# Reading the attention product and its maxima from PSUM, in a fused cross-attention and feed-forward kernel

## The reference, cut to what matters

```python
def reference(x, ctx_2048, W1, W2):            # x, ctx: 16 x 256 x 512 f32; W1 2048x512, W2 512x2048
    x = x + xattn(layernorm(x), ctx_2048, ctx_2048)
    x = x + ffn(layernorm(x), W1, W2)
    return x

def xattn(q, k, v):                            # 8 heads of 32 rows, over the 512 columns
    qk = einsum('bdm,bdn->bmn', qh, kh) / sqrt(32)
    return einsum('bmn,bcn->bcm', softmax(qk, axis=-1), vh)

def ffn(x, W1, W2):                            # both products with 8-bit rounded inputs, ternary weights
    h = silu(bitlinear(x, W1))
    return bitlinear(h, W2)
```

## Time and profile before

| | us |
|---|---|
| median of 3 runs | 919.39 (917.77 to 921.04) |
| the profiled execution | 921.06 |
| its span, first to last instruction | 919.0 |

### The profile page before, as it was taken

One profiled execution on the slowest core, in us unless ns is written; L12 is line 12 of the kernel. 1 busy time (PEld: TensorE's weight loads), 2 busy tenths in 40 slices (PEclk: granted clock), 3 DMA queues, 4 the chain that ended last, 5 costly groups with the idle time before them and its releaser, 6 DMA issues.

```text
span 919.0 us, 13936 instructions
## 1 busy us (share of the span) xinstructions
PE 791.9 (86%) x4580; PEld 292.9 (32%) x4580; DVE 789.7 (86%) x1624; ACT 671.6 (73%) x1089; POOL 617.5 (67%) x619
## 2 busy tenths in 40 slices
PE   1667799998999999999999999899999999989875
PEld 0322233333333333333333333333333333333222
DVE  1958799999999999999999999999999999998552
ACT  3485687877777777787777777787777778777753
POOL 4125578776777777777777777777777777875651
PEclk9977999999999999999999999999999999999997
DMA  8550333222333333312233333212233333120000
GB/s 264 156 158 18 70 81 70 61 63 63 71 81 81 82 81 70 82 47 65 63 81 81 82 81 81 70 50 67 60 79 81 81 82 81 47 58 25 24 12 23
DMA packets 49927, 68.28 MB, mean 74 GB/s; under 512 B 6336, under 2 KB 30912, under 8 KB 49344
## 3 DMA queue, kind: packets, MB, share of 16 engines
q1 hardware_dynamic: 49856, 67.39, 29.2%
HBM read 33.55 MB, written 8.39 MB: 46 GB/s over the span
## 4 chain that ended last, share of the span: by engine, by line
PE 51%; DVE 35%; issue 7%; POOL 3%; ACT 2%; DMA 1%; SPq 0%; POOLq 0%; ACTq 0%; DVEq 0%
PE bank_b L918 12%; DVE mx L703 11%; PE pv L887 9%; PE mxp L877 8%; PE st L867 7%; DVE hmx L782 6%; DVE late L777 6%; PE bank_b L956 4%; PE bank_a L956 3%; PE bank_a L908 3%; DVE cparts L713 2%; PE dn L898 1%; PE bank_a L926 1%; POOL late L492 1%; DVE sm L756 1%
## 5 line engine op out<-in xcount | busy, mean ns | idle before, releaser
L465 POOL TENSOR_TENSOR probs<-probs 128x512 f32<-128x512 f32 x256 | 332.8, 1317 | 138.5 <-PE pv L887 125.2
L703 DVE TENSOR_REDUCE mx<-mxp 128x1 f32<-128x512 f32 x512 | 338.1, 680 | 60.8 <-PE mxp L877 58.9
L546 ACT ACTIVATE probs<-st,sm 128x512 f32<-128x512 f32 x512 | 343.1, 686 | 53.0 <-PE st L867 49.8
L877 PE MATMUL mxp<-ks,qs 96*128 96x512 f16 x512 | 201.5, 395 | 56.8 <-DVE mx L703 24.9
L867 PE MATMUL st<-qs,ks 98*128 98x512 f16 x512 | 197.9, 388 | 5.3 <-DMA qs<-crow 3.1
L887 PE MATMUL pv<-probs,vt 128*32 128x512 f32 x1024 | 142.7, 630 | 0.0
L918 PE MATMUL bank_b<-w2t,late 128*128 128x512 f16 x512 | 134.7, 388 | 2.6 <-ACT late L578 2.6
L867 PEld LDWEIGHTS st<-qs,ks 98*128 98x128 f16 x512 | 50.1, 98 | 145.5 <-ACT probs L546 63.4
L877 PEld LDWEIGHTS mxp<-ks,qs 96*128 96x128 f16 x512 | 53.4, 105 | 132.1 <-DVE mx L703 65.2
L782 DVE TENSOR_REDUCE hmx<-late 128x1 f32<-128x512 f32 x128 | 84.6, 681 | 2.2
L609 ACT ACTIVATE late<-bank_a,sm 128x512 f32<-128x512 f32 x64 | 44.0, 688 | 50.4 <-PE bank_a L956 50.4
(11 more groups left out here) (92 smaller groups left out, 1024.9 us busy)
## 6 DMA issues: line engine op xcount, KB each, us to landing
xs<-x SPq DMA_DIRECT2D x32, 256.0 KB, 4.0
cs<-ctx SPq DMA_DIRECT2D x32, 256.0 KB, 4.1
ks<-kh SPq DMA_DIRECT2D x64, 128.0 KB, 3.4
qs<-qh SPq DMA_DIRECT2D x64, 128.0 KB, 3.7
xr<-x SPq DMA_DIRECT2D x32, 256.0 KB, 4.0
out<-late SPq DMA_DIRECT2D x32, 256.0 KB, 2.0
probs<-w SPq DMA_DIRECT2D x4, 1024.0 KB, 9.0
ks<-kl SPq DMA_DIRECT2D x32, 128.0 KB, 3.2
```

The lines of the kernel that those rows point to most:

```text
L465: pool.tensor_tensor(probs[:, 2 * pair, h, :], probs[:, 2 * pair, h, :], probs[:, 2 * pair + 1, h, :], ALU.add).then_inc(sum_done, 1)
L546: act.activation(probs[:, c, h, :], st[u % 2][:, :], ACT.Exp, scale=sm1[:, r, ESC:ESC + 1]).then_inc(exp_done, 1)
L703: dve.reduce_max(mx[:, slot.ring(off), NC * h + c:NC * h + c + 1], mxp[m % 2][:, :], axis=AX.X).then_inc(max_done, 1)
L877: pe.matmul(mxp[m % 2][:, :], qs[0:3 * DH, r, h, c * P:(c + 1) * P], ks[0:3 * DH, r, h, :], start=True, stop=True).then_inc(mx_done, 1)
```

## The change

- `values` c = 0 and 1 move from units 6 and 10 to units 8 and 11; `pv_evac` and `pvs` go, `attend` reads `pv`, and `values` c = 0 waits for `attended` of the tile before.
- `cparts` and `cparts_low` go. `mx` is 128 columns wide, zero beyond 16, and `ct` transposes it as f32, in unit 11 instead of 12. `ct_evac` writes the high part (f16) from bank_a, VectorE's new `ct_low` (unit 12) subtracts it from bank_a and writes the low part; bank_a is free after `ct_low`. The crow rows are two transfers.
- `sums` write a buffer of their own; they wait for `denominators` of the tile before instead of `values`. `exp` waits for `values` and for the sum that read its block.
- SyncE issues the loads first, then two transfers of `qh`, two of `kh`, one of `ql`, one of `kl`, each as soon as its half is ready.
- The memset of -1 goes from GpSimd (after the first `ql`) to VectorE's first instruction; `mx` is cleared by GpSimd at the start.
- `key_scale_b` is a tensor_scalar. Every step has its own semaphore, the leftovers of a loop form go (nothing is emitted for them before).

```diff
-    cparts=[-6],
-    ct=[-4],
+    ct=[-5],
     ct_evac=[-5],
-    values=[6, 10, 15, 18],
+    ct_low=[-4],
+    values=[8, 11, 15, 18],
-    pv_evac=[18],
...
+                if slot.has(4) and loads:
+                    load(slot, 4)
                 if slot.has(2):
-                    wait_alone(sp, st_done, slot, UNITS, 2 - RING, UNITS, passed)
-                    wait(sp, x_k_scales, slot, K_LOW, 2, K_LOW)
-                    for g, part in enumerate((kh, kl, kh)):
-                        sp.dma_start(ks[DH * g:DH * (g + 1), r, :, :], part[:, k, :]).then_inc(k_stacked[r], 16)
-                    wait(sp, x_k_operands, slot, Q_LOW, 2, Q_LOW)
-                    for g, part in enumerate((qh, qh, ql)):
-                        sp.dma_start(qs[DH * g:DH * (g + 1), r, :, :], part[:, k, :]).then_inc(q_stacked[r], 16)
+                    wait(sp, st_done, slot, UNITS, 2 - RING, UNITS)
+                    wait(sp, qh_done, slot, 1, 2, 1)
+                    for g in range(2):
+                        sp.dma_start(qs[DH * g:DH * (g + 1), r, :, :], qh[:, k, :]).then_inc(q_stacked[r], 16)
+                    wait(sp, kh_done, slot, 1, 2, 1)
+                    for g in (0, 2):
+                        sp.dma_start(ks[DH * g:DH * (g + 1), r, :, :], kh[:, k, :]).then_inc(k_stacked[r], 16)
+                    wait(sp, ql_done, slot, 1, 2, 1)
+                    sp.dma_start(qs[2 * DH:3 * DH, r, :, :], ql[:, k, :]).then_inc(q_stacked[r], 16)
+                    wait(sp, kl_done, slot, 1, 2, 1)
+                    sp.dma_start(ks[DH:2 * DH, r, :, :], kl[:, k, :]).then_inc(k_stacked[r], 16)
...
-                    wait(sp, ct_evac, slot, 1, 1, 1)
-                    sp.dma_start(qs[3 * DH:3 * DH + 2, r, :, :].rearrange("o h m -> o (h m)"), crow[:, k, :]).then_inc(c_stacked[r], 16)
+                    wait(sp, ct_low, slot, 1, 1, 1)
+                    for a in range(2):
+                        sp.dma_start(qs[3 * DH + a:3 * DH + a + 1, r, :, :].rearrange("o h m -> o (h m)"), crow[:, k, a, :]).then_inc(c_stacked[r], 16)
...
             def pair_sum(slot, off, n):
                 pair, h = divmod(n, TH)
                 if h == 0:
-                    wait_alone(pool, pv_done, slot, NC, off, 2 * pair + 1, passed)
+                    wait(pool, dn_done, slot, 2, off - 1, pair + 1)
                 wait(pool, exp_done, slot, UNITS, off, TH * (2 * pair + 1) + h + 1)
-                pool.tensor_tensor(probs[:, 2 * pair, h, :], probs[:, 2 * pair, h, :], probs[:, 2 * pair + 1, h, :],
+                pool.tensor_tensor(sums[:, pair, h, :], probs[:, 2 * pair, h, :], probs[:, 2 * pair + 1, h, :],
                                    ALU.add).then_inc(sum_done, 1)
...
-                if u % (2 * TH) == 0:
-                    wait(act, dn_done, slot, 2, -1, c // 2 + 1)
+                if h == 0:
+                    wait(act, pv_done, slot, NC, -1, c + 1)
+                wait(act, sum_done, slot, 2 * TH, -1, TH * (c // 2) + h + 1)
                 wait(act, st_done, slot, UNITS, 0, u + 1)
...
             def maximum_low(slot, off):
+                k = slot.ring(off) % 2
+                wait(dve, ct_evac, slot, 1, off, 1)
+                dve.tensor_tensor(crow[:, k, 1, :], bank_a[0:UNITS, 0:P], crow[:, k, 0, :], ALU.subtract).then_inc(ct_low, 1)
...
-                wait(dve, pv_evac, slot, 1, off, 1)
-                dve.tensor_tensor(att[:, k, :], pvs[:, k, :], rden[:, :], ALU.mult).then_inc(token_scales, 1)
+                wait(dve, pv_done, slot, NC, off, NC)
+                wait(dve, rden_done, slot, 1, off, 1)
+                dve.tensor_tensor(att[:, k, :], pv[:, :], rden[:, :], ALU.mult).then_inc(attended, 1)
...
+            dve.memset(ks[3 * DH:P, :, :, :], -1.0).then_inc(minus_ones, 1)
...
-                    wait(pe, pv_evac, slot, 1, off, 0)
+                    wait(pe, attended, slot, 1, off - 1, 1)
...
-                wait(pe, cpart_done, slot, 2, off, 2)
+                wait(pe, max_done, slot, UNITS, off, UNITS)
                 bank_free(pe, BANK_A, slot, off, place("ct", 0))
-                pe.transpose(bank_a[0:2 * UNITS, 0:P // 2].bitcast(f16), cparts[:, slot.ring(off), :, :].rearrange("p a b -> p (a b)"),
-                             idh[:, :]).then_inc(ct_done, 1)
+                pe.transpose(bank_a[:, 0:P], mx[:, slot.ring(off), :], idf[:, :]).then_inc(ct_done, 1)
```

More of the change, by code:

```diff
@@ L153, in wait @@
     value = slot.at(per_tile, off, more)
-    assert not slot.looped or per_tile * (slot.b + off) + more > 0
-    if slot.looped or value > 0:
+    if value > 0:
         engine.wait_ge(sem, value)
-def wait_alone(engine, sem, slot, per_tile, off, more, passed):
-    wait(engine, sem, slot, per_tile, off, more)
-    if slot.looped:
-        engine.sem_inc(passed, 1)
 def build(nc, x, ctx_in, w1, w2, out):
@@ L230, in build @@
         w2t = sb("w2t", [P, FG, D], f16)
-        mx = sb("mx", [P, RING, UNITS], f32)
-        cparts = sb("cparts", [P, RING, 2, UNITS], f16)
-        crow = sb("crow", [2 * UNITS, 2, P], f16)
+        mx = sb("mx", [P, RING, P], f32)
+        crow = sb("crow", [UNITS, 2, 2, P], f16)
         bn1 = sb("bn1", [P, RING, 6], f32)
@@ L358, in run @@
                     k = slot.ring(0) % 2
-                    wait_alone(sp, tokens, slot, T_QUANTISED, -2, RESIDUAL, passed)
+                    wait(sp, x1_done, slot, 1, -2, 1)
                     sp.dma_start(xr[:, k, :], x_t[slot.at(1, 0, 0), :, :]).then_inc(xr_loaded[k], 16)
@@ L524, in run @@
                                 steps[name](slot, off, *number)
-                    for at, step, *which in weights:
-                        if not slot.looped and at == UNITS * slot.b + u:
-                            step(*which)
             for b in range(-3, TILES + 2):
-                run(Slot(0, b, False))
+                run(Slot(b))
         @block.scalar
@@ L594, in maxima_evac @@
                 if slot.has(off - 2):
-                    act.wait_ge(c_stacked[slot.ring(off - 2)], slot.lap(off - 2, 16))
-                act.copy(crow[:, slot.ring(off) % 2, :], bank_a[0:2 * UNITS, 0:P // 2].bitcast(f16)).then_inc(ct_evac, 1)
+                    act.wait_ge(c_stacked[slot.ring(off - 2)], slot.lap(off - 2, 32))
+                act.copy(crow[:, slot.ring(off) % 2, 0, :], bank_a[0:UNITS, 0:P]).then_inc(ct_evac, 1)
             def tokens_evac(slot, off):
@@ L834, in run @@
             def run(slot):
-                steps = {"max_read": maximum, "cparts": maximum_parts, "cparts_low": maximum_low,
+                steps = {"max_read": maximum, "ct_low": maximum_low,
                          "hidden_scale": hidden_scale, "hidden_scale_b": hidden_scale_b,
@@ L848, in run @@
                     for at, step, *which in weights:
[L849 removed]
+                        if at == UNITS * slot.b + u:
                             step(*which)
             for b in range(-3, TILES + 2):
[L853 removed]
+                run(Slot(b))
         @block.tensor
         def _(pe):
[L857 removed]
+            pe.wait_ge(consts, 5)
             def scores(slot, u):
@@ L862, in scores @@
                 if u == 0:
-                    if not slot.looped and slot.b == 0:
-                        pe.wait_ge(consts, 5)
-                    pe.wait_ge(c_stacked[r], slot.lap(0, 16))
+                    if slot.b == 0:
+                        pe.wait_ge(minus_ones, 1)
+                    pe.wait_ge(c_stacked[r], slot.lap(0, 32))
                 wait(pe, exp_done, slot, UNITS, 0, u - 1)
@@ L893, in denominators @@
                 if pair == 0:
-                    if not slot.looped and slot.b + off == 0:
+                    if slot.b + off == 0:
                         pe.wait_ge(w_evac, WG)
-                    wait(pe, token_scales, slot, T_HIDDEN, off - 1, D_SPREAD)
+                    wait(pe, dn_spread, slot, 1, off - 1, 1)
                 for h in range(TH):
-                    last = pe.matmul(dn[DH * h:DH * (h + 1), :], ones[:, 0:DH], probs[:, 2 * pair, h, :],
+                    last = pe.matmul(dn[DH * h:DH * (h + 1), :], ones[:, 0:DH], sums[:, pair, h, :],
                                      start=(pair == 0), stop=(pair == 1), skip_group_check=True)
```

256 lines of the change are left out of this document (126 added, 130 removed).

## The result

The changed kernel takes 933.39 us (median of 4 runs, 932.76 to 933.79). The kernel before, on the same chip, takes 919.3 us. The ratio is 1.0152, with a 95% interval of 1.0139 to 1.0166: slower by 14 us. The profiled execution of the changed kernel took 932.76 us, its span is 931.0 us, 12.0 more than before.

What follows compares the result with a forecast made beforehand. A chain passing between TensorE, VectorE and GpSimd bounds each 25.71 us lap; 29 x 0.39 = +11.3, less 4.1 at start and end, is +7.2, giving 926.6 us. Own range 918 to 935, mostly 921 to 933; with rivals 907 to 937.

Steps and rivals of the forecast that it cites:

- The lost cover: TensorE, first half of the stage: values c=0 leaves unit 6, so `second` waits 0.83 us for ScalarE's evacuation.
- Rival A: Faster, 901 us: the 1.6 us of `cparts` pay and moving values c=0 doesn't cost; -0.5 us per slot; chance 0.16.
- Its test as written: First matmul of `second` at 458.1 us or later, released by ScalarE, would show the forecast right.
- The last maxima product: TensorE's maxima product of unit 10 comes 0.75 us later, at 464.84 instead of 464.09 us.
- A stall for a hole: TensorE, second half: `ct` waits near 0.5 us for a row maximum, both old holes go; net +0.39 us per slot.
- VectorE's stage: VectorE's last stage of the lap, from unit 0 to 4, only shifts and stays 8.0 us.
- rival C: Slower, 935 us: `ct_low` held up behind GpSimd's `finish` delays the token transpose, +0.27 x 29 = +8 us; chance 0.12.
- VectorE's work: VectorE ends up 2.4 us lighter per slot and stands near 77% busy.
- The start: Memset moved and transfers sooner: net -0.7 us; slots -1 to 1, crow rows sooner and `attend` on the chain: -2 us.
- The end: Last slot: the sum that waited 1.45 us for `values` no longer holds up residual and tokens, -1.4 us.
- Rival B: No change, 918 to 921 us: 0.15 to 0.2 us per slot, start and end give back 6 or more; chance 0.15.
- the sum: Slots 2 to 30: 29 x 0.39 = +11.3 us, less 4.1 for start and end, is +7.2 us.

## Why the prediction was right, and where it was short

The direction and the mechanism held, and the time lies in the range; the forecast of 926.6 us was 6.8 us too low. That the time still lies in the range, even in its inner part of 921 to 933 but for 0.4 us, is owed to the width that was given to the laps and the ends; nothing in it stood for a fall of the clock in the middle.

- **The lost cover held.** Predicted: `second` 1.71 us behind the first hidden transpose, released by ScalarE; measured 1.73 (486.89 to 488.62). The kernel with the copy kept shows it from the other side: with `values` back in unit 6 the hole is gone. The 0.83 us of the text were counted between starts, and so counted they are 0.84 (487.78 to 488.62); the row's 0.68 is counted from the modelled end. Rival A needed the lost cover not to cost, and a lap of 25.2; the hole opened by ScalarE and the lap of 26.08 decide against it. Its test as written, `second` at 458.1 or later, was wrong by the text's own sum, which had put it at 457.82; on that scale it came at 457.84.
- **The last maxima product** was to come 8.73 us behind the first transpose (464.84 less 456.11) and came 8.74 behind it (495.63). The last row maximum followed as worked out.
- **A stall for a hole held.** `ct` was predicted 9.96 us behind the first transpose and measured at 9.90. Between starts the hole before it is 0.51 us, near the 0.5 of the text; the row's 0.35 again counts from the modelled end. No row had stood behind the 0.05 us that I added for wider weights: from the end of the row maximum to `ct` it is 0.06 us, not 0.13. The token transpose was predicted at 12.93 and measured at 12.95. Per lap +0.39 predicted, +0.37 measured. The row after the change that confirms it best is the one without a note: the token transpose at 499.84 no longer waits for anything.
- **VectorE's stage was fixed.** From the row maximum at 504.86 to the next first hidden transpose at 512.97 it is 8.11 us, before it was 8.14 (473.68 to 481.82).
- **`ct_low`** was sized right, 0.27 us (0.25). It ended at 499.60, while GpSimd's `finish` ran from 498.47 to 499.75: it was not held up, so rival C fell. The Trainium skill's rule (SBUF — State Buffer, "Who interferes with whom"), that a VectorE instruction with at most one SBUF input and outside the two-port modes doesn't contend with GpSimd, agrees with this row.
- **`attend` had the right size for another reason.** Its mean is 0.679 us over 32 instead of 1.653, near the 0.7 of the text. But in 31 of the 32 no GpSimd step runs beside it any more: at 489.52 the pair sum had ended, at 489.04. The kernel with the copy kept reads `pvs` from SBUF and has the same 0.68 in 31 of 32. What both kernels share, and the kernel before lacks, is the sums' buffer with its waits: before, the sum stood waiting for `values` and so came to run beside `attend` (a row of GpSimd in the kernel before):

```profile
458.28 1.54 POOL L465 TENSOR_TENSOR probs<-probs 128x512 f32<-128x512 f32 x1 [1.27 <-PE pv L887]
```

Only the last but one `attend` still has a sum beside it, and there the place of the operand counts, 0.69 us from PSUM in the kernel after (first row) and 1.42 from SBUF in the one with the copy kept (second row), whose usual `attend` is the third:

```profile
878.85 0.69 DVE L724 TENSOR_TENSOR att<-pv,rden 128x512 f32<-128x512 f32 x1
```

```profile
846.96 1.42 DVE L733 TENSOR_TENSOR att<-pvs,rden 128x512 f32<-128x512 f32 x1
...
473.44 0.68 DVE L733 TENSOR_TENSOR att<-pvs,rden 128x512 f32<-128x512 f32 x1
```

So the saving that the text gave to PSUM came, in all but one tile, from GpSimd having left. That the number came out is luck; the time isn't touched by it, as the text says.
- **VectorE's work** fell by 1.8 us a slot, not 2.4. `attend` (-0.97) and the two `cparts` steps (-1.44) went as predicted, `ct_low` took 0.27, which is 2.14 less, near the 2.4; three terms were missing: the memset, 6.9 us once, `kl`, which has risen from 0.75 to 0.86 us, and the row maxima, 4.2 us more of busy time in all (one takes 0.683 instead of 0.680 us, and fewer overlap). With them the sum is -54 of the -57.7 us; 2.3 of the rest are in two weight steps at the start. So VectorE stands at 79% instead of the 77 of the text.
- **The start** gained 4.5 us instead of about 2.7, although the memset cost more than I took: it holds VectorE until 9.37 us, not 7.6, because it doesn't begin before 2.49. The first product came at 21.78, 0.85 later than before. The gain comes from the crow rows, whose wait is 1.48 us instead of 3.14, and from slots 0 and 1. The end gave 0.15 us, not the 1.4 predicted: the last slot but one took 22.93 instead of 22.50 us. Together, -4.1 was predicted and -4.5 to -6.1 came. Rival B needed as much given back, but with a lap sum of half of what came; it fell by the lap.

**The step that fell short is the sum.** It multiplies a lap by 29 and adds the ends, and takes TensorE's clock as granted between them. I used the clock once, in rival B, as something that the change could give back at the start. That new holes of TensorE might bring it down in the middle has no term in the sum, though the earlier trace rows show 0.50 just after TensorE had stood idle. Five falls cost 7.7 us, which is the whole of what was missed: 28 x 0.37 + 7.7 - 6.1 = 12.0. The run with the filled hole shows that this part is the clock and no wait.

What stays open: why the clock falls in every fourth lap of the kernel after between 247 and 698 us, in 11 and 12 laps of two others and in none of the profiled execution with `ct` in unit 12, all with the same hole of 0.68 us before `second`; and whether the filler works by its place or by its amount.

## What to carry to other kernels

Before a step of the tensor engine is moved, look at what stands idle on the other engines beneath it: here 1.03 us of products covered another engine's evacuation, and moving them turned a free evacuation into a hole that cost 0.85 us a lap. A change of several parts should be run part by part: here two parts gained 37 us together and the other two lost 50. And when an engine on the path gets new holes, put a term for its clock into the sum, and try cheap filler in the hole, which gave 8.7 us here.

## What the runs showed of the hardware

- The granted clock can fall for 3.4 us with TensorE 86% busy over the span and no single hole above 0.7 us in the lap. 96 filler matmuls of no use make the kernel faster by 8.7 us.
- The price of a fall depends on what TensorE would have waited for behind it: 1.5 us a lap in the kernel after, 1.1 with the old order of the transfers, 0.7 in the kernel before with values, `attend` and sums alone. In the last two, the wait of 0.8 to 1.0 us before the first maxima product is gone in the laps with a fall.
- One kernel can spread by 18 us from run to run (906.9 to 925.2, at mean granted clocks of 0.982 to 0.956), where the other kernels here spread by 1 to 8.
- A VectorE product of 128x512 f32 takes 0.68 us with no GpSimd step beside it, from PSUM (31 of 32 in the kernel after) or from SBUF (31 of 32 with the copy kept). Beside a pair sum it takes 0.69 us with one input in PSUM and 1.42 us with both in SBUF (one row each; the mean before, with a sum beside 29 of 32, is 1.65).
- VectorE writes -1 into 8192 f16 columns on 32 partitions in 6.88 us, GpSimd in 6.92:

```profile
2.49 6.88 DVE L658 MEMSET ks<- 32x8192 f16 x1 [2.49 <-issue]
```

The estimate from the Trainium skill (VectorE: DVE Perf Modes, "Zero memsets can be issued as uint32 (trn2)"), one cycle per element, was 8.5 us. The measurement decides: 0.84 ns per element of a partition.
